# An attention block with a rational softmax on one core: the diagonal packed into 68 equal pairs, two squares in one ScalarE instruction

## The reference

```
h      = x @ W_cond[id] + b_cond[id]                # one 512x512 weight per batch
q,k,v  = h @ w_qkv.T, 16 heads of 32 features
s      = q.k / sqrt(32) - slope * |i - j|,  -1e4 above the diagonal
num    = 0.5 * (1 + s * rsqrt(1 + s*s))             # in place of exp
o      = (num @ v) / (sum(num) + 1e-6)
x1     = x + o @ w_out.T
a      = relu(x1 @ W1 + b1) @ W2 + b2               # adapter, 512 -> 128 -> 512
z      = layernorm(x1 + a) * gamma + beta
out    = x1 + quantized(z) @ w8.T * scales + bias   # one scale: the largest |z| of both batches
```

## Time and profile before

| | |
|---|---|
| median of 3 runs | 2266.02 us (2264.18 to 2266.58) |
| the profiled execution | 2265.64 us, its span 2263.8 us |
| mean granted TensorE clock | 0.907 of full |
| PE busy | 1803.9 us, 80% |
| DVE busy | 1878.6 us, 83% |
| ACT busy | 1685.0 us, 74% |
| POOL busy | 1715.7 us, 76% |

### The profile page before, as it was taken

The page is one execution under the profiler, slowest core; times in us unless marked ns, Lnnn a source line. Parts: engine busy times, 40 slices in busy tenths (PEclk is TensorE's granted clock), DMA queues, the critical chain, the costliest instruction groups (busy, mean ns, idle before and its releaser), DMA issues.

```text
span 2263.8 us, 31228 instructions
## 1 busy us (share of the span) xinstructions
PE 1803.9 (80%) x10640; PEld 904.5 (40%) x10640; DVE 1878.6 (83%) x2114; ACT 1685.0 (74%) x1938; POOL 1715.7 (76%) x784
## 2 busy tenths in 40 slices
PE   5678877877787789998888877877787787887864
PEld 4555323333333346664444433333333333342331
DVE  4358888888889888889789898888888888899768
ACT  0247897989889888889567667999889888767413
POOL 2136887788878887788678887788878887788548
PEclk9899988988898899999999998988988898998879
DMA  5411111110111022202322221110111021121137
GB/s 176 146 49 44 49 30 35 43 45 25 40 40 49 20 69 66 68 25 74 84 77 81 69 54 34 40 49 21 45 40 48 20 79 44 42 62 52 59 123 237
DMA packets 126620, 138.68 MB, mean 61 GB/s; under 512 B 27868, under 2 KB 78044, under 8 KB 126044
## 3 DMA queue, kind: packets, MB, share of 16 engines
q1 hardware_dynamic: 126460, 136.64, 21.5%
HBM read 54.02 MB, written 22.80 MB: 34 GB/s over the span
## 4 chain that ended last, share of the span: by engine, by line
PE 38%; ACT 21%; DVE 20%; issue 12%; POOL 4%; DMA 2%; SPq 2%; DVEq 0%; POOLq 0%; ACTq 0%
ACT yb L669 9%; PE sc L825 7%; PE ov L804 7%; ACT yb L671 7%; DVE gb L1042 6%; PE dn L804 6%; ACT gb L661 6%; DVE gb L983 5%; PE it L723 5%; PE it L740 4%; PE it L747 4%; PE it L727 3%; POOL oT L654 2%; SPq L428 2%; PE it L707 1%
## 5 line engine op out<-in xcount | busy, mean ns | idle before, releaser
L623 POOL TENSOR_TENSOR yb<-yb 128x1024 f32<-128x1024 f32 (+3 forms) x640 | 1510.2, 2373 | 460.9 <-DVE gb L1042 448.6
L669 ACT ACTIVATE yb<-sc 128x1024 f32<-128x1024 f32 (+3 forms) x640 | 566.9, 886 | 376.3 <-PE sc L825 189.8
L1042 DVE TENSOR_TENSOR gb<-sc,yb 128x1024 f32<-128x1024 f32 (+3 forms) x640 | 676.6, 1057 | 186.1 <-ACT yb L671 183.9
L983 DVE TENSOR_TENSOR gb<-gb,yb 128x1024 f32<-128x1024 f32 (+3 forms) x640 | 779.2, 1218 | 3.9 <-ACT gb L661 0.5
L825 PE MATMUL sc<-qmv,kst 128*128 128x512 f32 (+3 forms) x1280 | 505.6, 472 | 295.8 <-DVE gb L1042 278.2
L671 ACT ACTIVATE yb<-yb 128x1024 f32<-128x1024 f32 (+3 forms) x640 | 595.0, 930 | 20.3
L661 ACT ACTIVATE gb<-gb 128x1024 f32<-128x1024 f32 (+3 forms) x640 | 584.1, 913 | 0.1
L825 PEld LDWEIGHTS sc<-qmv,kst 128*128 128x128 f32 x1280 | 238.7, 209 | 648.3 <-DVE gb L1042 453.3
L804 PE MATMUL ov<-gb,vv 128*32 128x512 f32 (+3 forms) x2560 | 338.4, 604 | 18.0 <-DVE den L997 10.5
L804 PE MATMUL dn<-gb,ones 128*32 128x512 f32 (+3 forms) x2560 | 326.3, 584 | 0.0
L723 PE MATMUL it<-hT,wT 128*128 128x512 f32 x496 | 249.9, 629 | 5.8 <-DVE area L921 1.8
(11 more groups left out here) (112 smaller groups left out, 1093.5 us busy)
## 6 DMA issues: line engine op xcount, KB each, us to landing
qmv<-stage SPq DMA_DIRECT2D x384, 64.0 KB
kst<-stage SPq DMA_DIRECT2D x384, 64.0 KB
area<-in_x_dram SPq DMA_DIRECT2D x58, 256.0 KB, 2.8
out_dram<-oT SPq DMA_DIRECT2D x32, 256.0 KB, 3.3
den<-rec_d SPq DMA_DIRECT2D x31, 256.0 KB
wT<-wT_d SPq DMA_DIRECT2D x7, 768.0 KB, 4.4
x_d<-area SPq DMA_DIRECT2D x16, 256.0 KB, 2.6
z_d<-area SPq DMA_DIRECT2D x16, 256.0 KB, 3.2
```

The lines of the kernel that those rows point to most:

```text
L623: pool.tensor_tensor(y, y, y, ALU.mult).then_inc(s_y2, 1)
L669: act.activation(y, sc[:, k % SLOTS, :, q0_of(g, k):], ACT.Square).then_inc(s_s2, 1)
L983: dve.tensor_tensor(t, t, yview(k)[:, :, q0:], ALU.add).then_inc(s_num, 1)
L1042: dve.tensor_tensor(gview(k)[:, :, q0:], sc[:, k % SLOTS, :, q0:], yview(k)[:, :, q0:], ALU.mult).then_inc(s_g, 1)
```

## The change

- The units on the diagonal are packed. Per chunk and for two heads at a time: key block 4c is whole (1024 columns); the blocks 4c+1 (384 queries) and 4c+3 (128 queries) share a tile of 512 columns a head; block 4c+2 (256 queries) of all four heads makes one pair. So a chunk's diagonal has 5 pairs of 1024 columns in place of 8 of four widths, with the same columns in sum, and a group has 68 pairs. Matmuls go piece by piece, as many as before and as wide.
- ACT's square of 1+g takes pairs n-2 and n-1 together, one instruction of 128x2048, behind each even pair n.
- The loops are gone: all 8 groups are written out.
- `rt`, `a` and `zt` are evicted by ACT, behind the pair at which the item stands; the largest |z| stays on DVE, a pair later. PE's and SP's waits for an eviction go by two semaphores, one for each engine.
- POOL's normalization becomes res*rstd + (-mean*rstd), with one more instruction on a 128x1 tile.
- The lags count pairs, LAG = 6 (as before in pairs), NORM_LAG = 3 and NORM_LAG_LAST = 1 (before 6 and 2). Each pair earns the planner the same PE time. Starts and ends of items go by the new pair numbers.
- A chunk's first pair waits for the chunk's q operand alone; its k operand is waited for at the chunk's first diagonal pair.

```
-        self.units = [(c, kb) for c in range(n_chunks) for kb in range(TT * (c + 1))]
+            for kb in range(TT * c):
+                unit(c, *both(c, (kb, 0)))
+            d = TT * c
+            unit(c, *both(c, (d, 0)))
+            unit(c, *both(c, (d + 1, P), (d + 3, 3 * P)))
+            unit(c, [Piece(h, d + 2, 2 * P, CH - 2 * P, h // 2, h % 2 * 2 * P) for h in range(HG)])
...
-            w = CH - self.width(k // 2)
-            left = max(-1.0, min(left, 0.5)) + (6 * w / 1200 + 0.5) - 1.35 * w / CH - 0.1 + slack
+            left = max(-1.0, min(left, 0.5)) + 6 * CH / 1200 - 0.95 + slack
...
-                t = gview(k)[:, :, q0_of(g, k):]
-                act.wait_ge(s_g, G * PAIRS + k + 1)
-                act.activation(t, t, ACT.Square, bias=1.0).then_inc(s_g2, 1)
+            def one_plus_g_squared(n):
+                both = gb[:, n % GRING:n % GRING + 2, :]
+                act.wait_ge(s_g, n + 2)
+                act.activation(both, both, ACT.Square, bias=1.0).then_inc(s_g2, 2)
...
+                    if n >= 2 and n % 2 == 0:
+                        one_plus_g_squared(n - 2)
+                    for job in after_pair.get(k, []):
+                        d = b if g is ending else b - 1
+                        after(d, job, bases[0] + job.index, zs_before(d, job.name[1]))
...
+                if what == "rt":
+                    act.activation(resT[a], feat, ACT.Copy).then_inc(s_evac_act, 1)
+                elif what == "a":
+                    act.activation(hid[a], bank[:, 0:P], ACT.Relu, bias=b1c[:, 0:1]).then_inc(s_evac_act, 1)
+                elif what == "zt":
+                    for k in range(KC):
+                        r = act.activation(resT[a][:, k, :], feat[:, k], ACT.Identity, scale=gam[:, k:k + 1],
+                                           bias=bet[:, k:k + 1])
...
+                    pool.tensor_scalar(shift[:, a:a + 1], mv[:, a, 0:1], rstd[:, a:a + 1], -1.0,
+                                       ALU.mult, ALU.mult).then_inc(s_rstd[a], 1)
...
-                        if kb == 0 and k % 2 == 0:
+                        for what, at in (("q", g.first[c]), ("k", g.first[c] + 2 * TT * c)):
+                            if k == at:
```

More of the change, by code:

```diff
@@ L105, in __init__ @@
         for c in range(n_chunks):
[L106 removed]
+            p0, p1 = self.first[c], self.last[c]
             if c < n_chunks - 1:
@@ L177, in adaln_attn_ffn @@
     plain = Group(NC, [], True)
-    first = [2 * u for u in plain.first] + [2 * len(plain.units)]
+    first = plain.first + [len(plain.pairs)]
     opening = Group(NC, [job for j in range(TT, KB)
@@ L207, in runs @@
     def runs(b):
-        return [(0, opening if b == 0 else joining, 1), (1, plain, NG - 2), (NG - 1, ending if b == B - 1 else closing, 1)]
-    starts, n = {}, PRO
+        return ([(0, opening if b == 0 else joining)] + [(hg, plain) for hg in range(1, NG - 1)] +
+                [(NG - 1, ending if b == B - 1 else closing)])
+    starts, n = {}, (PRO, PRO, 0)
     for b in range(B):
-        for hg, g, count in runs(b):
+        for hg, g in runs(b):
             starts[b, hg] = n
-            n += count * len(g.items)
-    REST = n
+            n = tuple(v + w for v, w in zip(n, (len(g.items), g.evacs["dve"], g.evacs["act"])))
+    REST, REST_DVE, REST_ACT = n
     PRO_JOBS = woven(cond_jobs, range(TT))
     END_JOBS = woven(after_jobs, range(DONE, KB), KB - DONE)
+    END_ITEMS = [job for job in END_JOBS if job.parts]
+    END_RANKS, END_EVACS = ranks(END_ITEMS)
     PLACES = 2 + KB - DONE
@@ L411, in ops_before, with zs_before @@
             return 2 if g is opening else 2 * NC * G + 3
+        def zs_before(b, j):
+            order = [job.name[1] for job in (ending if b == B - 1 else joining).items if job.name[0] == "zt"]
+            n = KB * b
+            return n + (order.index(j - 2) + 1 if j >= 2 else 0)
         @block.sync
@@ L553, in group @@
                     elif what in ("o", "zt"):
-                        after(b if g is ending else b - 1, e[1], base + item)
+                        after(b if g is ending else b - 1, e[1], base + item, (act_base if what == "zt" else dve_base) + rank)
                     item += 1
-            for_groups(sp, group)
+            for_groups(group)
             sp.wait_ge(s_pv, B * NG * UNITS)
```

399 lines of the change are left out of this document (230 added, 169 removed).

## The result

The changed kernel takes 2275.11 us (median; 2268.22 to 2282.94) beside 2264.9 us for the kernel before (2258.46 to 2270.35): 1.0044 times as long, interval 1.0035 to 1.0053, so slower by 0.4%. I had forecast 2139 us and a range from 2080 to 2210; it lies outside. The profiled execution has a span of 2272.7 us at a granted clock of 0.913, before 2263.8 at 0.907.

A forecast was written before the change was run, and what follows sets the result against it. ACT was taken to bound plain groups, DVE joining and ending, PE closing. Span 94 + 274 + 4 x 215 + 239 + 291 + 255 + 123.8 = 2136.8 us, plus 1.8: forecast 2139, range 2080 to 2210.

The forecast's parts named there:

- part 3: Plain groups' stalls: of 27 us, 13 go with the narrow pairs; 14 stay, 18.5 with the double square's.
- part 2: ACT's double square: fewer starts save 4.3 us a plain group, against 3 to 6 us of new stalls.
- part 4: Evictions moved from DVE to ACT: joining group 291 us (-25), bound by PE; ending group 255 us (-26).
- part 1: Packing, 12 pairs fewer a group: ACT 4.5 us less, DVE 198 to 195, POOL 191 to 181, PE nothing.
- rival E: The double square's loop sets the pace: a plain group 244 us, the whole 2287; chance 0.05.
- rival C: DVE's sum and POOL's square can't run together: 3.23 us a pair, the whole 2210; chance 0.05.
- part 5: Groups bound by PE: closing 239 us (-1), opening 274 us (-6).
- part 7: SP's queue: DVE could stand up to 4.6 us for the reciprocal's DMA behind an operand; taken as 0.
- rival B: DVE waits for the reciprocal's DMAs behind operands in SP: +56 us, the whole 2195; chance 0.18.
- part 6: Small things: loops written out 0, POOL's further instruction +2 us, zt on ACT -2, later k wait 0.
- rival F: Relu or copy needs another ACT table: loads cost 7.7 us a tile, the whole 2313; chance 0.03.

The follow-up runs named there:

- a1_single: The changed kernel with ACT's square of 1+g taken pair by pair again, all else as changed: 2233.73 us, 0.9867 times before.
- d2_div_early: a1_single with DVE's division of a chunk's output one pair earlier: 2212.31 us, 0.9786 times before.
- b1_double: The kernel before with only the double square added: 2401.31 us, 1.0594 times before.
- a3_dve_evict: The changed kernel with rt, a and zt evicted by DVE again: 2281.76 us, 1.0069 times before.

## Why the prediction was wrong

It named 2136.8 us of span and 2272.7 came, 136 more. By the spans of the profiled executions 46 belong to the double square, about 40 to the stalls of the plain groups, 37 to the joining group, 10 to the opening one and 4 to the end; start, closing and ending give 1 back. (The 46 are 41 by the medians: the profiled execution of a1_single was the quickest of its four.) Two steps failed most: part 3, by which half of the stalls would go, and part 2, by which the double square would cost nothing net; the joining group of part 4 is the third.

**Packing (part 1) held as far as it went.** The counts are as forecast, and a plain group keeps ACT busy for 198.8 us (forecast 196.5), DVE for 200 (195) and POOL for 188 (181). In plain groups the changed kernel with single squares wins 7 us (232.1 to 225.0). Packing was not run alone, so these 7 are those of packing, the shorter lags and the new places of the items together; that the place of the division counts is shown by d2_div_early.

**The stalls (part 3) did not halve.** This step failed. I took the loss of chunk 0 for the narrow pairs' own, since chunk 3 with as many of them lost as much. 14 us were to stay without the double square's part, and with single squares 25 of ACT's idle time (226 - 201) stay of the 27. Chunk 0 did lose most of its own: in a1_single the four chunks of a plain group have 2.7, 5.3, 6.8 and 9.8 us of it on the mean, before 7.2, 4.7, 7.1 and 7.8. So chunk 0 wins 4.5, chunk 3 loses 2.0 although its narrow pairs are gone too, and the double square adds 3.0 more there. My guess is that in chunk 3 the narrow pairs had been the room in which ACT and DVE caught up; no run shows it. That two chunks lose alike did not show where the loss arises, only that it does not grow with length in that order of work. The runs name one piece of what stayed, the heap on DVE at a chunk's end (d2_div_early), and leave the rest open.

**The double square (part 2, rivals C and E) was mis-sized, and its mechanism too.** I set 3 to 6 us of stalls against 4.3 of saved starts: no net price. It costs 46 us of span (2272.7 against 2227.1), 15 of them in the opening group. The saving was too large: ACT's busy time falls by 16 us over eight groups, 2.0 a group (in whole pairs without a stall two pairs take 5.80 us in place of 5.89). And the waits were far too small: 61 us. Two things make them. First, the double square has to wait until g of its second pair is there. Each heap on DVE in front of that g holds it, 36.5 us in all; I had looked for lumps in front of the sum only. Second, the sum. I had reckoned the loop at 5.27 us with a sum of 1.37, the mean over all pairs. The double square makes the sum late; where POOL has begun by then, the sum takes up to 2.9 us, and a loop with a sum of 2.5 to 2.9 is 6.4 to 6.8 us, over the 5.78 that ACT needs. In the kernel before this is common (52 of 112 sums of even whole pairs in its plain groups are over 2.4 us with the double square), in the changed kernel rarer (15 of 136). With POOL's square cut short the double square costs the packed kernel nothing. So the runs bear out the mechanisms of both rivals together: I had priced the loop of rival E and the lock of rival C each alone, and refused both. Pricing E with the lock of C was the step that I left out.

**C's lock is there.** I argued from POOL's 2.81 against 2.01 us that the two overlap in part. The b1_double rows above have DVE's sum standing until POOL's square ends: it ends 1.08 us behind it, near its own undisturbed 1.22. It works the other way too, in the changed kernel's timeline (the same POOL instruction, first alone, then with a sum of DVE beside it):

```profile
1203.55 0.77 POOL L665 TENSOR_SCALAR area<-area,rstd,shift 128x512 f32<-128x512 f32 x1
...
1209.56 1.22 DVE L1066 TENSOR_TENSOR gb<-gb,yb 128x1024 f32<-128x1024 f32 x1
...
1209.59 1.83 POOL L665 TENSOR_SCALAR area<-area,rstd,shift 128x512 f32<-128x512 f32 x1
```

1.06 us more, near a sum's undisturbed 1.22. The whole trace of the changed kernel says the same: of the sums that come up inside a square of POOL's with over 0.2 us of it left (239), every one ends 1.08 us behind that square, and of the squares that come up inside a sum with over 0.3 us left (468), every one ends 1.75 us behind that sum; the shortest squares take 1.89. So 0.8 us in the earlier trace rows was the part of a full block that fell inside the square (the sum beside it ends at 647.89, the square at 649.65, 1.76 later), not a mild one. The Trainium skill ("SBUF — State Buffer", section Who interferes with whom) calls the port pair that the two share an exclusive lock. The traces here agree: 1.06 of 1.22 us one way, 1.62 us added the other.

Nor did the cadence of 2.94 us speak against it. When the two take turns, each runs some 0.14 us of its length beside the other's end, so a pair costs 1.75 + 1.08 = 2.83 us and not 2.01 + 1.22 = 3.23: just under the 2.94 that ACT needs. In the kernel before, the lock fits into ACT's cadence with 0.1 us to spare, and a later sum breaks that order.

**Evictions (part 4).** ACT took them at the price reckoned (`zt` 455 ns, `rt` 583, `a` 352, DVE 283 to 253 in the joining group, where I had 238), and the ending group with single squares is 254.8 for 255 forecast. That is luck: I had built 255 as a plain group of 215 and 40 more, and it is one of 225 and 30 more. Yet a3_dve_evict shows that most of its gain isn't the move's (4 us of 20, at the edge of the scatter); the rest comes with the other parts of the change, which were not run apart. Joining failed: I took PE for the next bound at 288 us. With single squares and the load off SP's queue it is 317.2, no less than before. PE is busy for 268.8 of those us (85%) and no engine for more, so no engine's load explains the 317; the burst at pairs 20 to 22 is one visible piece of what does. What would remove it stays open; higher credits than 1.2 were not run.

**Opening and closing (part 5).** Single squares put them at 283.5 and 240.9, against 274 and 239. The 6 us that the opening group was to gain never came; no run shows why, and part 3's reason is my guess.

**Queues (part 7, rival B).** DVE waits 13.7 us for the reciprocal's DMA where it waited 1.6: the mechanism is there at a quarter of its price. The same queue hit harder where I hadn't looked, at the residual's x: 10 to 11 us. I had counted only the queue's items that the change moves; the x load wasn't moved, its neighbour was.

**Small things (part 6) and rival F.** The end takes 128.1 us with single squares for 123.8 forecast. Its start is late: counted from the last pair (2 us behind the start of its last square), the last division begins at 14.4 us in place of 6.8, and the first of the six last normalizations at 42.2 in place of 34.3. The shorter normalizations win part of it back: the sixth begins at 50.9 in place of 47.9. a3_dve_evict has 131.1, so the evictions on ACT are not the cause; the last pairs are now whole where they were narrow, which would fit, but was not run. Loops written out: 0.9984. Relu, copy and the scaled copy on ACT need no further table: the two loads at the first pair are still the only ones.

## What to carry to other kernels

Before two small instructions are made one, look at what its consumer meets when it comes one instruction later: a consumer that shares a port with another engine may have lost its turn, and pays for the rest of that engine's instruction. Look as well at how long the joined instruction waits for the second of its inputs. Two objections that are each too small alone must also be priced together. Equal stalls in unequal chunks do not show that the narrow part causes them; taking the narrow part away can leave most of them in place. When work is packed, look at every in-order queue (SP's here) for loads that now stand behind a long block of others, not only at the items that were edited.

## What the runs showed of the hardware

- On POOL a normalization of 128x512 written as (x - mean) * rstd took 2.34 us (joined groups) and 2.08 (the end); as x * rstd + shift it takes 1.42 and 0.77. So the new form is less than half as long where no pairs run, and 0.6 of the old one among the pairs, where DVE's sums stretch it; it needs one 128x1 instruction of 0.40 us more. The two forms differ in the operations and in one of the two 128x1 operands, and which of these counts was not run:

```profile
L665 POOL TENSOR_SCALAR area<-area,rstd,shift 128x512 f32<-128x512 f32 x26 | 36.8, 1416 | 2.6
...
L662 POOL TENSOR_SCALAR shift<-mv,rstd 128x1 f32<-128x1 f32 x32 | 12.9, 404 | 3.3
...
L665 POOL TENSOR_SCALAR yb<-yb,rstd,shift 128x512 f32<-128x512 f32 x6 | 4.6, 772 | 0.6
```

- DVE's sum of 128x1024 takes 1.22 us undisturbed. When it comes up inside POOL's square it ends 1.08 us behind that square, so that it takes up to 2.9, and its length in the profile holds that standing: a mean over both kinds (1.37 before) is the length of neither. POOL's square ends 1.75 us behind a sum in which it comes up. Taking turns, the two need 2.83 us a pair.
- With most of the products for `dn` left out the granted clock of a plain group fell from 0.91 to 0.84, and the score matmul of 512 columns grew from 491 to 540 ns: leaving this work out gave back 15 us of PE's time where 29 were meant.
